# The last normalization moved into the experts' block, its residual added by TensorE

## What is computed

```
out = 0.5 * gelu(flat @ shared_W + shared_b)
for e in range(8):                                   # top 2 of 8 experts have a weight above 0
    h = gelu(flat @ W1[e] + b1[e])
    out = out + combine[:, e:e + 1] * (h @ W2[e] + b2[e])
mean, var = out.mean(-1), ((out - mean) ** 2).mean(-1)
out = (out - mean) * rsqrt(var + LN_EPS) * gamma + beta      # first normalization of the last stage
x = layernorm(x + out)                                       # second normalization of the last stage
```

## Time and profile before

| | us |
|---|---|
| median of three runs | 2039.67 |
| the profiled execution | 2050.05 |
| its span | 2048.4 |
| last matmul of `experts` to first load of `outputs` | about 1969 to 1984.76 |
| `outputs`, first load to the end of the span | 1984.76 to 2048.4 |

### The profile page before, as it was taken

The page is one execution under the profiler, slowest core; times in us unless marked ns, Lnnn a source line. Parts: engine busy times, 40 slices in busy tenths (PEclk is TensorE's granted clock), DMA queues, the critical chain, the costliest instruction groups (busy, mean ns, idle before and its releaser), DMA issues. The chain is left out here.

```text
span 2048.4 us, 30761 instructions
## 1 busy us (share of the span) xinstructions
PE 1837.0 (90%) x10808; PEld 1167.9 (57%) x10808; DVE 1322.6 (65%) x1719; ACT 958.9 (47%) x1452; POOL 322.7 (16%) x339
## 2 busy tenths in 40 slices
PE   1999999999999999999999999589829999999940
PEld 1544544444444445444444444477619999999940
DVE  3577776777777777767767777233385656666537
ACT  3555454455545455545455455022315545555426
POOL 0000000000000000000000000000006666766643
PEclk9999999999999999999999999899969999999975
DMA  7000000000000000000000000444133323333343
GB/s 261 11 21 17 26 21 16 26 21 16 27 18 19 27 16 21 27 16 21 24 19 21 23 15 16 175 166 171 43 128 83 85 51 93 64 82 87 85 93 102
DMA packets 73077, 115.41 MB, mean 56 GB/s; under 512 B 7563, under 2 KB 47693, under 8 KB 70669
## 3 DMA queue, kind: packets, MB, share of 16 engines
q1 hardware_dynamic: 55949, 90.92, 12.9%
q0 software_dynamic: 17024, 23.12, 6.3%
HBM read 75.44 MB, written 38.57 MB: 56 GB/s over the span
## 5 line engine op out<-in xcount | busy, mean ns | idle before, releaser
L418 ACT ACTIVATE a_e<-banks 128x1024 f32<-128x1024 f32 x512 | 496.4, 1022 | 212.9 <-PE banks L334 212.8
L478 DVE TENSOR_TENSOR a_esum<-a_esum,a_e 128x1024 f32<-128x1024 f32 x384 | 469.4, 1222 | 57.3 <-ACT a_e L418 36.1
L348 PE MATMUL banks<-a_e,a_v 128*64 128x512 f32 x2048 | 495.7, 605 | 0.0
L348 PEld LDWEIGHTS banks<-a_e,a_v 128*64 128x64 f32 x2048 | 124.1, 136 | 238.7 <-issue 176.1
L334 PE MATMUL banks<-a_qh,a_kh 64*128 64x512 f32 x1024 | 229.0, 444 | 2.0 <-DVE a_ql L466 1.6
L482 DVE RECIPROCAL a_inv<-banks 128x512 f32<-128x512 f32 x64 | 214.9, 3358 | 15.5 <-PE banks L357 15.5
L475 DVE TENSOR_TENSOR a_esum<-a_e 128x1024 f32<-128x1024 f32 x64 | 78.4, 1225 | 201.6 <-ACT a_e L418 201.6
L334 PE MATMUL banks<-a_qh,a_kl 64*128 64x512 f32 x1024 | 201.5, 390 | 0.0
L334 PE MATMUL banks<-a_ql,a_kh 64*128 64x512 f32 x1024 | 200.9, 389 | 0.0
L59 POOL MEMSET t_ident<- 128x128 f32 x1 | 0.2, 204 | 1259.9 <-POOLq L192 1259.9
L1409 ACT ACTIVATE e_g<-banks,e_b1c 128x256 f32<-128x256 f32 x280 | 113.2, 471 | 151.9 <-PE banks L1357 151.1
(11 more groups left out here) (213 smaller groups left out, 2827.1 us busy)
## 6 DMA issues: line engine op xcount, KB each, us to landing
attn_out<-a_ot SPq DMA_DIRECT2D x64, 256.0 KB, 2.0
t_ot<-attn_out SPq DMA_DIRECT2D x8, 2048.0 KB, 8.2
a_w<-w_qkv SPq DMA_DIRECT2D x32, 256.0 KB, 3.1
up<-w_up SPq DMA_DIRECT2D x8, 1024.0 KB
down<-w_down SPq DMA_DIRECT2D x8, 1024.0 KB
b_xr<-x_rows SPq DMA_DIRECT2D x4, 1024.0 KB, 12.7
raw<-x_t SPq DMA_DIRECT2D x8, 512.0 KB, 10.4
t_xr<-x_rows SPq DMA_DIRECT2D x8, 512.0 KB, 9.0
```

What stands on the lines that cost most here:

```text
L348: mm = pe.matmul(o_acc[slot % 2][h * DH:(h + 1) * DH, :], v[quad % 2][:, n, head], e[n % NE][:, h * BANK:(h + 1) * BANK], start=n == 0, st ...
L418: act.activation(e[n % NE], ring[n % 2], ACT.Exp, scale=SCALE).then_inc(e_ok, 1)
L478: dve.tensor_tensor(acc[:, :], acc[:, :], e[n % NE], ALU.add).then_inc(add_ok, 1)
```

## The change

- `outputs` is no stage of its own any more. It returns five functions, which `experts` calls at the end of each engine's list, in the same block. SP's waits for a new semaphore, `all_stored`, which POOL raises in `end` right after its wait for `y_out`.
- The loads go into the buffer `shared` instead of a buffer of their own. Gamma is loaded ahead of the wait for `all_stored`.
- The groups are 2, 4, 4, 4, 4, 4, 4, 4, 2 tiles: nine instead of eight.
- `mix` is done by PE: for a pair of tiles, one product of the identity with `x2b` and one of the identity with `y` (already multiplied by gamma) add up in one of PSUM's banks 0 to 3. The second statistics and the second normalization read PSUM. The mean and variance move to banks 4 and 5.
- POOL multiplies by gamma in pairs of tiles (128x512 instead of 128x1024).
- The second half of a group follows two groups behind the first (LAG = 2).

```
-        experts(nc, banks, keep, w_up, w_down, x2_rows, acc_rows, w_rows)
-        outputs(nc, banks, keep, gamma, acc_rows, out)
+        experts(nc, banks, keep, w_up, w_down, x2_rows, acc_rows, w_rows, gamma, out)
...
             def end(c):
                 gp.wait_ge(y_out, 16 * CT * c)
+                gp.nop().then_inc(all_stored, 1)
...
+    SIZES = [2] + [4] * ((TT - 4) // 4) + [2]
+    PAIR = 2
+    LAG = 2
...
+    def sync(sp):
+        sp.dma_start(g[:, :], gamma.partition_broadcast(P)).then_inc(c_in, 16)
+        sp.wait_ge(all_stored, 1)
+        for k in range(GROUPS):
+            sp.dma_start(y[:, TILES[k], :], rows[:, TILES[k], :]).then_inc(rows_in[k], 16)
...
+    def gpsimd(gp):
+        gp.memset(eps[:, 0:1], 4.0 * EPS).then_inc(eps_ok, 1)
+        gp.memset(eps[:, 1:2], EPS).then_inc(eps_ok, 1)
+        gp.wait_ge(c_in, 16)
+        for k in range(GROUPS):
+            for t in pairs(k):
+                gp.wait_ge(norm_ok[0], t + PAIR)
+                gp.tensor_tensor(y[:, t:t + PAIR, :], y[:, t:t + PAIR, :],
+                                 g[:, :].unsqueeze(1).to_broadcast([P, PAIR, D]), ALU.mult).then_inc(scaled, 1)
+
+    def tensor(pe):
+        flat = lambda rows, t: rows[:, t:t + PAIR, :].rearrange("p t d -> p (t d)")
+        for t in range(0, TT, PAIR):
+            n = t // PAIR
+            if n == 0:
+                pe.wait_ge(norm_ok[0], 1)
+            if n >= 4:
+                pe.wait_ge(norm_ok[1], t - 4 * PAIR + PAIR)
+            pe.matmul(mix_bank(t)[:, :], ident[:, :], flat(x2b, t), start=True, stop=False)
+            pe.wait_ge(scaled, n + 1)
+            pe.matmul(mix_bank(t)[:, :], ident[:, :], flat(y, t), start=False, stop=True).then_inc(mixed, 1)
...
+        act.wait_ge(eps_ok, 2)
+        act.activation(warm[:, :], eps[:, 0:1], ACT.Sqrt)
+        for k in range(GROUPS + LAG + 1):
+            if k < GROUPS:
+                deviation(0, k)
+            if k > LAG:
+                normalize(1, k - LAG - 1)
+            if k < GROUPS:
+                normalize(0, k)
+            if LAG <= k < GROUPS + LAG:
+                deviation(1, k - LAG)
...
+        for k in range(GROUPS + LAG + 1):
+            if k < GROUPS:
+                statistics(0, k)
+            if k > LAG:
+                inverse(1, k - LAG - 1)
+            if k < GROUPS:
+                inverse(0, k)
+            if LAG <= k < GROUPS + LAG:
+                statistics(1, k - LAG)
```

More of the change, by code:

```diff
@@ L13 @@
+import itertools
 from contextlib import ExitStack
@@ L1189, in experts @@
+def experts(nc, banks, keep, w_up, w_down, x2_rows, acc_rows, w_rows, gamma, out):
     x2, numbers, plan, w1, w1h, w1l, w2, b1all, b2all, beta_rows = (keep[n] for n in (
@@ L1225, in experts @@
                                      "y_done", "y_ok"))
-        y_out, y_stored = sem("e_y_out"), sem("e_y_stored")
+        y_out, y_stored, all_stored = sem("e_y_out"), sem("e_y_stored"), sem("e_all_stored")
+        outputs_sync, outputs_gpsimd, outputs_tensor, outputs_scalar, outputs_vector = outputs(
+            nc, ctx, banks, keep, ident, all_stored, gamma, acc_rows, out)
         block = ctx.enter_context(nc.Block())
@@ L1308, in _ @@
             all_chunks(gp, chunk, end, peeled=1)
+            outputs_gpsimd(gp)
         @block.sync
@@ L1337, in _ @@
             all_chunks(sp, chunk, end)
+            outputs_sync(sp)
         @block.tensor
@@ L1383, in _ @@
             all_chunks(pe, chunk)
+            outputs_tensor(pe)
         @block.scalar
@@ L1430, in _ @@
             all_chunks(act, chunk)
+            outputs_scalar(act)
         @block.vector
@@ L1482, in _ @@
             all_chunks(dve, chunk)
[L1485 to L1600, removed]
-                if k:
-                    inverse(1, k - 1)
-                mix(k)
-                if k + 1 < GROUPS:
-                    inverse(0, k + 1)
-                statistics(1, k)
-            inverse(1, GROUPS - 1)
@@ L1610 @@
+            outputs_vector(dve)
 class Banks:
```

64 lines of the change are left out of this document (63 added, 1 removed).

## The result

| | before | after |
|---|---|---|
| median of the runs, us | 2038.73 (2037.02 to 2039.78, 4 runs) | 2016.75 (2014.92 to 2017.66, 4 runs) |
| ratio after : before | | 0.9892, 95% interval 0.9875 to 0.9909 |
| profiled execution: span | 2048.4 | 2015.2 |
| last accumulating DMA issued by POOL | 1973.56 | 1962.55 |
| first load of the last stage | 1984.76 | 1966.45 |

The changed kernel is 22.0 us (1.1%) faster; the forecast was 2018.5. The two profiled spans differ by more, 33.2 us, but 11.0 of these lie ahead of the last accumulating DMA, in code that is the same in both. By this measure the change is worth 74.84 - 52.65 = 22.2 us: 7.3 between the issue and the first load (11.20 to 3.90), 14.9 from there to the end (63.64 to 48.75).

What follows compares the result with a forecast made beforehand. Bound by the order of the round, DVE nearest to full. The stage, 47.0 + 3.0 = 50.0 us from 1977.2, ends at 2027.2 instead of 2048.4, 21.2 less; 2039.67 - 21.2 = 2018.5, range 2014 to 2026.

Steps and rivals of the forecast that it cites:

- The block end: Between experts' block and last stage: SP's wait ends at 1977.2 instead of 1984.76, gain 7.5 us (7.2 to 7.7).
- Gamma and the first load: Start of the last stage: 256 KB instead of 512 KB lands in 3.4 us instead of 4.09; gamma's issue free.
- The round: Full group of the last stage: ACT is the bound at 4.44 us, 4.5 with handovers; DVE 4.02.
- PSUM as a source: Reading PSUM: bn_stats 0.00 to 0.04 us more, taken as 0, ACT 0.04 less; by the skill's prices 2020.2.
- PE's start and its waits: PE's half-clock start of the last stage costs 1.0 us (0 to 2); bank waits cost nothing at full clock.
- the clock falls at times: Rival, last stage: PE at half clock for half of the time, rounds of 5.2 us, 4.5 back, 2023; 12%.
- The list as a whole: ACT's steps from SP's first load: first normalize(0) at 5.0, last at 45.8; 47.0 with handovers and PE's start.
- The end: From the last normalization to the end of the span: 3.0 us instead of 3.69, as 256 KB land sooner.
- The DRAIN at the end: POOL's DRAIN, were it 7.0 us again, runs from t of about 40 to 47, hidden by 3 us.
- POOL's debt: Rival, start of the stage: POOL's next instruction pays the 7.0 us, memsets at about 1984.5, 4.6 back, 2023; 7%.
- half clock throughout: Rival: PE at half clock all through the last stage, 1.72 us a product, 2034.9; 4%.
- slow products with exposed weight loads: Rival, last stage: PE at half clock, each product with its start 2.04 us, 5.5 later than before, 2045.2; 3%.

Runs made afterwards that it cites:

- e2_own_block: The changed last stage put back into a block of its own behind the block end; 2037.84 us, ratio 0.9934 to the kernel before.
- e4_even: The changed kernel with eight groups of 4 tiles instead of 2, 4 x 7, 2; 2033.11 us, ratio 0.9913 to the kernel before.
- e10_pool_share: The changed kernel with POOL taking one first normalization of each group of four from ACT; 2014.00 us, ratio 0.9888 to the kernel before.
- e6_pe_three: The changed kernel with one more identity product per pair, into a bank nobody reads; 2023.48 us, ratio 0.9928 to the kernel before.
- e7_dve_mix: The changed kernel with the residual added by DVE and no PE work in the stage; 2023.18 us, ratio 0.9924 to the kernel before.

## Why the prediction was right, step by step

*The block end* (7.5, bounds 7.2 to 7.7): 7.3 in the pair of traces, 7.4 with the block end alone. Right, and the 7.0 of the DRAIN is the reason: it comes back whole in e2_own_block.

*Gamma and the first load* (3.4): 2.8. The landing was over-counted by 0.6; e4_even shows the other size, 3.84, so two tiles save 1.05, more than their bytes.

*The round* (4.44, with handovers 4.5): 4.48. Term by term: the two deviations with the wait for the inverse 0.70 (0.66 said), `normalize(1)` from PSUM has its four starts in 1.82 (1.81 said), `normalize(0)` 1.96 (1.97), DVE 4.07 (4.02 said), POOL 2.49 (2.4 to 2.6), PE 3.70 with its starts (3.44). That ACT is the bound is shown by e10_pool_share, where less for ACT makes the round shorter; that PE and DVE lie just beneath is shown by e6_pe_three and e7_dve_mix. One figure of the prediction is wrong: it calls 16% of DVE's round free, which is about what the old round leaves (9.98 of 12 us busy); in the new one its own 4.02 of 4.5 leave 11%, and 9% were measured. It did no harm, as the prices from PSUM were small.

*PSUM as a source*: bn_stats 418 ns from PSUM and 408 from SBUF, ACT 563 and 596. The 0.01 and 0.04 of rows 6 carried over to other instructions. The Trainium skill (VectorE: DVE Perf Modes, "The TRN2 errata") has 62 cycles more for VectorE, 0.065 us. This trace does not bear that out (0.010), and the estimate of 2020.2 by it is 3.4 us too high, 1.7 of them by this term. The Trainium skill's 52 cycles less for ScalarE are 0.043, near the 0.033 here.

*PE's start and its waits* (1.0 for the start, the bank wait at no cost): here the size was nearly right and the place wrong. In the first trace three products go at half clock at the start, but DVE waits only 0.25 us for them (1979.95), and the list ends at 46.2 (2012.66 - 1966.45) where I had 47.0. The microsecond is spent elsewhere: counted from the landing, the turn that opens the full rounds comes at 14.5 where I had 13.6, and but for the 0.25 that is DVE's own list and its handovers with ACT in the first turns. That the allowance fitted is partly luck. In the other two traces the list ends at 47.1 and 47.2, but PE's start was quicker in both; the microsecond went to the bank wait, which I had put at nothing. I had looked at PE's rest in a full round only, 1.1 us said and 0.78 measured, and not at its first one, where nothing but the bank wait holds it: 1.52 to 2.07. My rival "the clock falls at times" was there, once in the stage instead of half of it.

*The list as a whole*, in us from the first load, said and measured: first `normalize(0)` 5.0 and 4.6; `normalize(1, 0)` 12.9 and 12.8; next turn 17.0 and 17.4; after four full rounds 35.0 and 35.3; then 38.5 and 38.8, 42.3 and 42.7, 44.8 and 45.2. It is 0.4 early at the first entry, by the landing, and 0.4 late at the last: 0.8 in 40 us, against the 1.2 that the sum adds behind these entries for PE's start and handovers.

*The end* (3.0): 2.5; the last store lands in 2.2 us. *The DRAIN at the end* (hidden by 3 us): hidden by 1.9. POOL's last product ended at 39.5, where I had said 40, but SP had seen the last store at 48.5, where I had said 50.

Together: 21.2 said, 22.2 measured in the traces and 22.0 by the medians. The extra microsecond is the first load 0.6, the list from its landing to the last normalization 0.2 (43.6 said, 43.4 measured) and the end 0.5, less 0.3 at the block end. In the two later traces the stage takes 49.8 and 49.7 from its first load, close to the 50.0 said; there the bank wait's microsecond stands against the first load and the end that I had over-counted, so that this agreement is luck as well. The chosen way from one execution to the median (carry the 10.4 over) held, as 11.0 us of the two spans' difference lay ahead of the stage.

Of the rivals, POOL's debt fell with the memset at 0.42 us, and half clock throughout and the slow products with exposed weight loads with the 0.86 between products.

## What to carry to other kernels

When a long round has three engines in a row and none full, put the later half of the work far enough behind that each engine's list stands alone, and then move work from the longest list to the engine that is idle; here the first step, with POOL's products in pairs, brought 0.67 us a round and the second 0.92. Count an idle engine's price at both of its clocks, and look for its longest rest, not its mean one: here that was near the start, at the first wait for a bank. Look at what lies between two blocks for a DRAIN that waits for no data, and move it to where something longer covers it.

## What the runs showed of the hardware

POOL's DRAIN behind the experts' indirect DMAs takes 7.0 us whenever it comes: 7007 ns at the block end in three kernels, and 7.0 behind POOL's last product when the stage of 40 us stood between them, long after the last of these DMAs had landed. One indirect gather alone doesn't cause it.

Of PE's clock the stage showed these pairs: behind rests of 1.24, 1.39, 1.52 and 1.84 us the next product of 512 columns took 1.1 to 1.2 by its record and the ones after it 1.02 (full clock, 2.4 GHz); behind rests of 2.06, 2.07, 2.10 and 2.12 the next three had one to three at 1.7 to 2.1 (half clock, 1.2 GHz). The 1.77 of rows 8, with full clock behind it, fits the first list. The rests between 1.84 and 2.06 are not covered, and what PE did ahead of a rest differs from case to case, so these pairs are no rule.
